# Converting expert weights to bf16 in the value-projection stage instead of the attention stage

## The reference

```python
xn = _layernorm(x, axis=-1)
# attention, one head of 1024
xq = einsum('bsd,ed->bse', xn, wq); xk = ...(xn, wk); xv = ...(xn, wv)
xq = apply_rotary(xq, cos, sin);    xk = apply_rotary(xk, cos, sin)
scores = einsum('bqd,bkd->bqk', xq, xk) / sqrt(D)
attn_out = einsum('bsd,ed->bse', softmax(scores) @ xv, wo)
# experts: 16 routed of width 256 (top 2), 2 shared of width 512
comb = one_hot(top2 of softmax(flat @ router_w)) * normalised weights
h = silu(flat @ wg_r[e]) * (flat @ wu_r[e]) * comb[:, e]
ffn_out = sum_e h[e] @ wd_r[e] + sum_n (silu(flat @ wg_s[n]) * (flat @ wu_s[n])) @ wd_s[n]
return x + attn_out + ffn_out
```

## Time and profile before

| | us |
|---|---|
| median of 2 timed runs | 4227.48 (4226.52 to 4228.44) |
| the profiled execution | 4230.61 |
| its span (core 6, the slowest) | 4229.1 |
| the other cores' spans | 4170.5 to 4228.2 |
| PE busy (share of the span) | 3501.0 (83%) |
| VectorE, ScalarE busy | 1470.9 (35%), 609.1 (14%) |

### The profile page before, as it was taken

The page is one execution under the profiler, slowest core; times in us unless marked ns, Lnnn a source line. Parts: engine busy times, 40 slices in busy tenths (PEclk is TensorE's granted clock), DMA queues, the critical chain, the costliest instruction groups (busy, mean ns, idle before and its releaser), DMA issues.

```text
span 4229.1 us, 49627 instructions; the slowest of 8 cores (4170.5 to 4229.1 us)
## 1 busy us (share of the span) xinstructions
PE 3501.0 (83%) x15904; PEld 1520.5 (36%) x15904; DVE 1470.9 (35%) x3681; ACT 609.1 (14%) x1507; POOL 63.9 (2%) x126
## 2 busy tenths in 40 slices
PE   4665936778787878787878689999999999999998
PEld 1222412333333333333333234444444444444443
DVE  4664012343434343443343331323223232323231
ACT  3332301111111111111111010111101010101010
POOL 0000030000000000000000000000000000000000
PEclk8777967899898999899989799999999999999999
DMA  5445199710101010101010254343433444434242
GB/s 142 157 160 160 60 141 118 88 55 6 56 6 53 8 53 8 53 6 55 6 46 6 58 164 144 140 145 136 148 138 142 140 150 139 159 120 179 100 170 90
DMA packets 121452, 412.60 MB, mean 98 GB/s; under 512 B 22752, under 2 KB 33248, under 8 KB 98800
## 3 DMA queue, kind: packets, MB, share of 16 engines
q1 hardware_dynamic: 105808, 361.15, 25.2%
q0 software_dynamic: 14240, 39.89, 7.5%
q10 hardware_dynamic: 1152, 8.39, 0.5%
HBM read 415.57 MB, written 58.85 MB: 112 GB/s over the span
## 4 chain that ended last, share of the span: by engine, by line
PE 70%; DMA 11%; DVE 8%; issue 5%; ACT 4%; POOL 1%; DVEq 0%; another core or an unknown queue 0%; SPq 0%; ACTq 0%; POOLq 0%
PE pb L101 70%; DMA f_wd<-wdr_bf 4%; DMA wgu_bf<-wgu 3%; DVE d_sc L101 2%; DMA b_x<-x 2%; ACT d_P L101 2%; DMA attn_sp<-d_at 1%; DVE b_st L101 1%; DVE d_OT L101 1%; POOL d_wqT L101 1%; ACT d_sc L101 1%; DMA f_xnt<-xn_sp 1%; DVE d_qfm L101 1%; DVEq L98 0%; DVE b_kswp L101 0%
## 5 line engine op out<-in xcount | busy, mean ns | idle before, releaser
L101 PE MATMUL pb<-f_xnt,f_wgu 128*128 128x512 bf16 x4096 | 906.9, 380 | 34.0 <-DMA f_xnt<-xn_sp 33.7
L101 PE MATMUL pb<-Vs,d_PT 128*128 128x512 bf16 x2048 | 549.3, 406 | 93.6 <-DVE d_PT L101 93.6
L101 PEld LDWEIGHTS pb<-f_xnt,f_wgu 128*128 128x128 bf16 x4096 | 392.0, 98 | 518.9 <-issue 63.8
L101 PE MATMUL pb<-Kfm,d_qfm 128*128 128x512 bf16 x2048 | 467.0, 390 | 64.9 <-DVE d_qfm L101 47.1
L101 PE MATMUL pb<-f_wd,f_h 128*128 128x512 bf16 x2048 | 464.2, 385 | 43.9 <-DMA f_wd<-wdr_bf 29.9
L101 DVE SCALAR_TENSOR_TENSOR f_uu<-pb,f_cb 128x512 bf16<-128x512 f32 x256 | 176.9, 691 | 570.7 <-PE pb L101 570.7
L101 DVE CAST d_PT<-pb 128x128 bf16<-128x128 f32 x1024 | 289.3, 290 | 232.1 <-PE pb L101 231.5
L101 ACT ACTIVATE f_sg<-pb 128x512 bf16<-128x512 f32 x256 | 152.8, 597 | 1323.7 <-PE pb L101 1310.2
L101 PEld LDWEIGHTS pb<-Kfm,d_qfm 128*128 128x128 bf16 x2048 | 202.9, 100 | 319.7 <-issue 95.3
L101 PEld LDWEIGHTS pb<-f_wd,f_h 128*128 128x128 bf16 x2048 | 196.3, 99 | 311.9 <-issue 98.5
L101 PEld LDWEIGHTS pb<-Vs,d_PT 128*128 128x128 bf16 x2048 | 171.4, 103 | 243.1 <-issue 127.7
(11 more groups left out here) (87 smaller groups left out, 2281.9 us busy)
## 6 DMA issues: line engine op xcount, KB each, us to landing
f_wgu<-wgu_bf SPq DMA_DIRECT2D x128, 1024.0 KB, 4.9
f_wd<-wdr_bf SPq DMA_DIRECT2D x128, 512.0 KB, 3.5
b_x<-x SPq DMA_DIRECT2D x32, 512.0 KB, 5.2
b_ct<-ctab SPq DMA_DIRECT2D x64, 256.0 KB, 3.2
b_stl<-stab SPq DMA_DIRECT2D x64, 256.0 KB, 3.8
d_ct<-ctab SPq DMA_DIRECT2D x64, 256.0 KB, 3.0
d_stl<-stab SPq DMA_DIRECT2D x64, 256.0 KB, 3.1
wgu_bf<-wgu POOLq DMA_DIRECT2D x16, 1024.0 KB, 29.6
```

What stands on the lines that cost most here:

```text
L101: inst = getattr(eng, meth)(*args, **kw)
```

## The change

The 32 conversions are written in `phase_b2`, behind the loads of `wvT`, instead of in `phase_d`, behind those of `woT`. The tokens for which stage F waits are taken there too.

```diff
@@ -470,6 +470,10 @@  (phase_b2)
                                self.wT_d["wvT"][:, c * D + h * 512:
                                                 c * D + h * 512 + 512])
                               for c in range(NCH)]) for h in range(2)]
+        for e in range(NE):
+            self.gload([(self.wgu_bf[e], self.wgu_d[e])])
+            self.gload([(self.wdr_bf[e], self.wdr_d[e])])
+        self.tok_conv = [self.P.tok("dG%d" % i) for i in range(NGS)]
 
         for tt in range(self.NTT):
@@ -548,10 +552,6 @@  (phase_d)
         tok_wo = [self.gload([(woTh[h][:, :], self.woT_d[h])])
                   for h in range(2)]
-        for e in range(NE):
-            self.gload([(self.wgu_bf[e], self.wgu_d[e])])
-            self.gload([(self.wdr_bf[e], self.wdr_d[e])])
-        self.tok_conv = [self.P.tok("dG%d" % i) for i in range(NGS)]
         t0m = P.op("V", "memset", nmp[:, :], 0.0, inc="V")
```

## The result

| | before | changed |
|---|---|---|
| median | 4227.5 us | 4288.9 us |
| ratio of the times, 95% interval | | 1.0148 [1.0132, 1.0164] |
| the profiled execution's span | 4229.1 (core 6) | 4289.7 (core 2) |
| shortest span of a core | 4170.5 | 4259.1 |

The change costs 61 us; 57 were forecast (4285).

A forecast was written before the change was run, and what follows sets the result against it. Conversions, running at what the DMA engines give, were taken to delay stage D's first-tile tables. Stage D starting 125 us later, less 68 us back, gives +57 on 4230.6; less 3 for the median, 4285, range 4257 to 4318.

The forecast's parts named there:

- Parts 1 and 2: POOL issues 32 conversions before stage D's loads; stage D waits for projection end or last conversion, whichever is later.
- Part 3: Stage B2: 25.17 MB of conversions at 102 to 107.8 GB/s; stage D starts at 655, 125 us later.
- the prediction's signs: Readings named beforehand as showing it right or wrong, such as stage D's first work at 655 to 662.
- Part 4: Stage B2: `c_xnt` tiles land 28.3 us apart, projection ends at 616 to 630, cover 25 to 39 us, no cost.
- Rival B: Starved projection in stage B2: `c_xnt` tiles 45 us apart, stage D starts about 683; +85 us, 4312; chance 0.06.
- Part 5: Stage D's first query tile, without conversions beside its tables, takes 252 us instead of 320.4: 68 us back.
- Part 6: Query tiles 2 to 8 and stage F see no conversion in either kernel: nothing.
- A: Conversions run quicker in stage B2: no change in time at 134 GB/s, 4207 us at 150 GB/s; chance 0.05.
- C: The wait before stage D doesn't bite, its tokens satisfied early: start at 630, +40 us, 4268; chance 0.02.
- D: Projection and conversions slow each other in stage B2, 92 GB/s throughout: +94 us, 4321; chance 0.09.

The follow-up runs named there:

- e1: The changed kernel with the conversions on four semaphores of their own, outside the wait between stages B2 and D: 4291.7 and 4292.7 us.
- e8: The changed kernel with the conversions on their own semaphores and stage D's weights loaded in stage B2 ahead of them: 4310.7 us.
- e2: The changed kernel with each `c_xnt` tile loaded in two DMAs of half the columns: 4337.8 us.
- e9: The changed kernel with every second `c_xnt` tile ordered on ScalarE's DMA queue instead of SP's: 4295.1 us.
- e4: The kernel before, with all conversions in stage D put behind the rotation of the first query tile: 4193.6 us.
- e5: The kernel before, with four conversions behind the rotation of each of stage D's eight query tiles: ratio 0.9808, single times 4153 to 4159 us.
- e6: e5 with `d_woTh` too loaded behind the first query tile's rotation: 4137.4 us.

## Why the prediction was right

The prediction held, at 4285 against 4288.9, with the right mechanism and two terms off by a few us in opposite directions.

*Parts 1 and 2, the wait.* Right: on core 2 the first work of SP, VectorE and POOL in stage D comes at 662.7 to 663.2, and the releaser named is a conversion; PE's comes at 670.08, behind its weights. But the wait was called the cause, in the end of the sum, as if it stood alone ("a barrier stands behind that stretch"). e1 shows that behind it POOL's order, which part 1 mentions and then prices at nothing, holds stage D as long, and that SP's slow `d_xnt` would by itself hold it nearly as long. e8 shows that slowing with both gates open.

*Part 3, the conversions.* Stage D was to start 655 - 397 = 258 us after stage B2; it was 264.9 on core 2 and 264.8 on the mean. The rate was nearly right. The table of stretches and POOL's queue in the changed kernel, 430 to 600, when `c_wvT` is through:

```profile
430.00:600.00 170.00, 99.56 (x400) 42.45 (x407) 0.00 (x0) 29.86 (x51) 10.85 (x22) 0.77 1.01 136
```

```profile
q0 software_dynamic: 875, 17.14, 86.1%
```

17.14 MB in 170 us is 100.8 GB/s, against the 102 read from the earlier trace rows; on the other cores it is 97 to just under 100, a little under the 100 to 110 that the prediction's signs allowed. Towards the end, with the last tile landing at 612, it is higher (6.98 MB in 600 to 660, 116 GB/s), and over 425 to 662 it is 104. Of the 7 us that were missing, 3.7 are `c_wvT`, whose last part landed 24.9 us after its first issue instead of 21.2 (422.75 - 397.84 against 418.13 - 396.97). Behind its last slices the first two conversions are now queued. The other runs bear this out as the cause: on the mean over the cores the last part lands 22.4 to 23.7 us after the stage's start in the kernels with all conversions behind it (changed, e1, e2, e9) and 19.6 to 20.6 in those with nothing behind it (before, e4, e5, e6). I had let the conversions be delayed by `c_wvT` and not the other way round. The rest is within the estimates for the beginning and the last landing. Two signs came late, where 655 to 662 were given for both: `d_rws` at 663.2, by these 7 us, and the first router matmul at 670.08, since it comes 7 us behind stage D's start in either kernel.

*Part 4, the projection under cover.* Right: tiles 28.9 us apart (28.3 forecast), the end 231.7 us after the stage's start (219 to 233), 33 us of cover left. The reading that the time of such a transfer doesn't hang on its bytes was taken from one case; e2 confirms it with twice the rows. The limit of 38 us between tiles, from which on the projection would decide, was added up wrongly: with the last tile landing at 432 + 6 x 38 = 660 the cover is long gone. It goes when 25 to 39 us are spread over six tiles, at 28.3 plus 4 to 6.5, so from 33 to 35 us on. Rival B was thus nearer than the prediction took it to be.

*Part 5, what is given back.* 72.8 us from core to core instead of 68. The scores came at 57 instead of 65. `d_woTh` costs the scores 10.7 us (57.8 in e5, 47.1 in e6, which differ in it alone) and not 14.5. The two bounds were a start of the scores at 50.5 (83 us back) and at 75 (58 back); the truth lay nearer to the lower, and e6, which is the case of that bound, came 3 us under it.

*Part 6.* Right: stage F 1812.2 us before and 1811.8 now on the mean of the cores.

*The rivals.* A faster stream (A) did not come: 100.8 GB/s where 134 were needed. The Trainium skill (HBM Reference, Specifications (TRN2), where its figure stands) gives a core about 358 GB/s with both cores of a pair streaming; an end 22 us earlier was the estimate from it. That did not come either: 100.8 GB/s written and twice that read are 302 together. Starvation (B) needs tiles 33 to 35 us apart and was then seen at 57, in e2. C and D did not happen.

*What the prediction did not see* is that core 6 was not typical. The give-back differs from core to core, as the first tile did before: 280 to 325 us, now 245 to 251. A change that makes a stall vanish gives the slowest core more than the mean, 73 against 59; the sum was made on the slowest core and so came out right for the maximum. There is luck in that. Core 6 itself went from 4229.1 to 4271.0, 42 us and not 61: its stage B2 grew by 132.0 and its stage D shrank by 75.4, but its stages B1 and F also came out 5.4 and 9.2 us shorter in that execution, which no part of the change explains. Core 2 became the slowest, with B1 and F as long as core 6 had had them. And the 7 us that the delay was short and the 5 that the give-back was short cancel in part. Why the stall differed between the cores before wasn't tried.

## What to carry to other kernels

Before a block of transfers is moved into a stage with idle DMA engines, compare its length (here 240 us) with what is free there (112 us), and look at what is behind it: each wait that counts its semaphore, each load in its queue, and each small transfer that runs beside it. Opening one of these gates moves the cost to the next (e1; for e8 the waits for `d_xnt` and the tables). A long stream that nobody needs soon is best cut into pieces and tied to points of the program at which no small transfer is due: e5 hides the same 25 MB completely, for a line of waits.

## What the runs showed of the hardware

- Beside a stream of large DRAM-to-DRAM transfers with a change of type on POOL's queue, a transfer of 128 rows on SP's queue lands 28 to 29 us after the one ahead of it, whether its rows have 2 KB or 8 KB; twice the rows took 57 (e2). With nothing ahead in its queue, 1 MB in 128 rows took 31 to 41 us from order to landing (31.1 in the changed kernel, 38.2 in e1, 38.5 in e8, 40.4 in e9). On a free queue the 8 KB rows take 4.8 us.
- SP's queue moved one packet for each packet of the stream (96 and 96 in 20 us; 100 and 100 with half rows). A second queue got a turn of its own: 47, 48 and 46 packets in 10 us, and SP's and ScalarE's together 77 GB/s against 39 for SP's alone (e9).
- The stream itself, with all eight cores doing the same, ran at 97 to 101 GB/s at its destination beside the `c_xnt` tiles, 102 beside the tables and 108 with hardly anything beside it.
